# Cross-attention block in fp32 on one core: output projection pair by pair over both tiles, and another order of copies, row sums and one product in the last two attention steps

## The reference, cut to what matters

```python
# x: (2, 2048, 512)  context: (2, 77, 512)  mask: (2, 2048, 77)  H = 16 heads of D = 32
q = layer_norm(x, qn_w, qn_b) @ q_w
k, v = split(layer_norm(context, cn_w, cn_b) @ kv_w)
attn = softmax(where(mask, -FLT_MAX, q . k * D**-0.5))     # per head, 77 keys
x = x + (attn . v) @ proj_w + proj_b
h = gelu(layer_norm(x, n2_w, n2_b) @ fc1_w + fc1_b) @ fc2_w + fc2_b      # 512 -> 2048 -> 512
return x + h
```

## Time and profile before

| | |
|---|---|
| median of three executions | 1068.85 us (1067.42 to 1070.12) |
| the profiled execution, its own time | 1066.18 us |
| its span, first to last instruction | 1064.4 us |
| TensorE busy in the span | 97% |
| VectorE busy | 78% |
| mean granted TensorE clock | 0.995 |

### The profile page before, as it was taken

The page is one execution under the profiler, slowest core; times in us unless marked ns, Lnnn a source line. Parts: engine busy times, 40 slices in busy tenths (PEclk is TensorE's granted clock), DMA queues, the critical chain, the costliest instruction groups (busy, mean ns, idle before and its releaser), DMA issues.

```text
span 1064.4 us, 16336 instructions
## 1 busy us (share of the span) xinstructions
PE 1037.7 (97%) x5857; PEld 856.4 (80%) x5857; DVE 834.3 (78%) x1323; ACT 434.0 (41%) x766; POOL 356.5 (33%) x259
## 2 busy tenths in 40 slices
PE   8999999999999989999999999999999999999998
PEld 6787788888888767887778888887888888888887
DVE  7888989999898789888887666677776677666655
ACT  4343334544434555454453333442433443223221
POOL 2455566665778645232614000302200120400000
PEclk8999999999999999999999999999999999999999
DMA  7012112211210065744477435435635433834312
GB/s 263 9 45 70 50 54 84 86 60 61 80 62 22 21 237 193 262 169 158 180 294 258 184 125 214 157 131 193 261 118 194 161 121 146 316 119 178 113 76 80
DMA packets 52279, 149.19 MB, mean 140 GB/s; under 512 B 10801, under 2 KB 19033, under 8 KB 44019
## 3 DMA queue, kind: packets, MB, share of 16 engines
q1 hardware_dynamic: 51627, 147.25, 38.4%
q10 hardware_dynamic: 584, 1.06, 0.3%
HBM read 108.13 MB, written 39.85 MB: 139 GB/s over the span
## 4 chain that ended last, share of the span: by engine, by line
PE 67%; DVE 18%; DMA 6%; issue 5%; POOL 3%; ACT 1%; DVEq 0%; SPq 0%; POOLq 0%; ACTq 0%
PE bank L1789 28%; PE bank L1759 25%; PE bank L1638 6%; DMA xr<-in_x 3%; DVE xhat L1208 3%; DMA x_scratch<-xr 2%; PE bank L1593 2%; DVE nmax L1160 2%; DVE esum L1185 2%; PE bank L1574 1%; DVE S L1153 1%; DVE aTl L1180 1%; DVE bnst L1196 1%; DVE hring L1374 1%; PE bank L1768 1%
## 5 line engine op out<-in xcount | busy, mean ns | idle before, releaser
L1789 PE MATMUL bank<-w2r,gT 128*128 128x512 f32 x1536 | 360.0, 391 | 2.6 <-DVE acc L1398 2.4
L1789 PEld LDWEIGHTS bank<-w2r,gT 128*128 128x128 f32 x1536 | 286.7, 188 | 64.8 <-DVE acc L1398 6.0
L1759 PE MATMUL bank<-hop,w1r 128*128 128x512 f32 x1344 | 313.5, 392 | 1.3 <-POOL w2r L776 1.3
L1759 PEld LDWEIGHTS bank<-hop,w1r 128*128 128x128 f32 x1344 | 252.5, 189 | 54.5 <-issue 2.1
L1398 DVE TENSOR_TENSOR acc<-bank,acc 128x512 f32<-128x512 f32 x256 | 176.5, 691 | 103.1 <-PE bank L1789 98.3
L1385 DVE TENSOR_TENSOR ybuf<-bank,ybuf 128x512 f32<-128x512 f32 x224 | 148.3, 688 | 71.6 <-PE bank L1759 67.2
L1036 ACT ACTIVATE ybuf<-ybuf,cols 128x512 f32<-128x512 f32 x128 | 91.7, 716 | 162.9 <-DVE ybuf L1385 162.9
L1390 DVE TENSOR_TENSOR gT<-ybuf,gT 128x512 fp32r<-128x512 f32 x128 | 101.7, 816 | 0.0
L676 POOL TENSOR_TENSOR S<-S,rsum 128x1232 f32<-128x1232 f32 x32 | 74.4, 2326 | 63.6 <-DVE rsum L1190 63.6
L641 POOL TENSOR_TENSOR hrs<-hve,mhalf 128x1 f32<-128x1 f32 x32 | 18.0, 562 | 220.1 <-DVE hve L1370 220.1
L669 POOL TENSOR_TENSOR S<-S,nmax 128x1232 f32<-128x1232 f32 x32 | 72.1, 2252 | 35.7 <-DVE nmax L1160 35.4
(11 more groups left out here) (111 smaller groups left out, 1432.0 us busy)
## 6 DMA issues: line engine op xcount, KB each, us to landing
w1r<-w_scratch SPq DMA_DIRECT2D x24, 1792.0 KB, 7.3
w2r<-w_scratch SPq DMA_DIRECT2D x24, 1024.0 KB, 5.2
w_scratch<-w1r SPq DMA_DIRECT2D x8, 1792.0 KB, 6.3
xr<-in_x SPq DMA_DIRECT2D x16, 512.0 KB, 4.1
x_scratch<-xr SPq DMA_DIRECT2D x16, 512.0 KB, 2.8
hring<-x_scratch SPq DMA_DIRECT2D x32, 256.0 KB, 3.0
acc<-x_scratch SPq DMA_DIRECT2D x32, 256.0 KB, 3.8
w_scratch<-w2r SPq DMA_DIRECT2D x8, 1024.0 KB, 9.1
```

The lines of the kernel that those rows point to most:

```text
L1759: mm = pe.matmul(bank_[:, :], w1r[:, w1_slot(s), c, w, kk * P:(kk + 1) * P], hop[i][:, d, kk, :], start=(kk == 0 and n == 0), stop=(kk == ...
L1789: mm = pe.matmul(bY[t % 2][:, :], gT[s % 2][:, j, d, t * P:(t + 1) * P], w2r[:, s % 2, j, w, :], start=(n == 0), stop=(n == 5))
```

## The change

TensorE: `proj` takes the pair as well, and a step runs pair 0 of tile 0, pair 0 of tile 1, pair 1 of tile 0, pair 1 of tile 1 (six matmuls each, in all 24 as before); the banks of both tiles are open at once, and tile 0 is announced as done after the 18th matmul, where it was after the 12th. This holds for all 16 steps. In step 15 the first feed-forward product M1 stands ahead of `prob_T(0)`.

ScalarE, step 14: `prob_out(1)` stands ahead of `exp_all(0)`, where it stood behind it (in step 15 nothing lies between the two places).

VectorE, step 14: `exp_sum(0)` and `recip(0)` ahead of `av_lo(1)`, where they were behind it; `w1_lo(0, 0)` right behind `av_lo(1)`, ahead of `exp_sum(1)`; `hop_lo(0, 1)` ahead of `residual(0)`, where it was between the two residuals.

```diff
@@ ScalarE, step
             if back and (tail == 1 or tail == 2):
                 av_hi(0)
+                prob_out(1)
             if scores:
                 exp_all(0)
             if back and not (tail == 1 or tail == 2):
                 av_hi(0)
-            if back:
                 prob_out(1)
@@ VectorE, step
             if tail == 1:
+                exp_sum(0)
+                recip(0)
                 av_lo(1)
+                w1_lo(0, 0)
...
-            if scores:
+            if scores and tail != 1:
                 exp_sum(0)
                 recip(0)
...
             if tail == 1:
-                w1_lo(0, 0)
+                hop_lo(0, 1)
...
             if back:
                 residual(0)
-            if tail == 1:
-                hop_lo(0, 1)
@@ TensorE, step
-            def proj(t):
+            def proj(pair, t):
                 bank_ = proj_bank(t, scores)
-                if t == 0 and scores:
+                if pair == 0 and t == 0 and scores:
                     v_scores.wait(pe, s, UT * KT - 1)
-                terms = [(c, w, d) for pair in range(PR) for lo in (HI, LO) for c in (2 * pair, 2 * pair + 1)
-                         for w, d in PRODUCTS if d == lo]
+                terms = [(c, w, d) for lo in (HI, LO) for c in (2 * pair, 2 * pair + 1) for w, d in PRODUCTS if d == lo]
                 for n, (c, w, d) in enumerate(terms):
                     if t == 0 and c % 2 == 0 and w == HI:
-                        (a_av, v_av)[d].wait(pe, b, c // 2)
+                        (a_av, v_av)[d].wait(pe, b, pair)
                     mm = pe.matmul(bank_[:, :], aT[d][:, c, t * P:(t + 1) * P], wp[w][:, c, :],
-                                   start=(n == 0), stop=(n == len(terms) - 1))
-                mm.then_inc(t_proj.sem, 1)
+                                   start=(pair == 0 and n == 0), stop=(pair == PR - 1 and n == len(terms) - 1))
+                if pair == PR - 1:
+                    mm.then_inc(t_proj.sem, 1)
...
+            if tail == 2:
+                mul(0, 0, M1, first=True)
             if back:
                 prob_T(0)
             if tail == 2:
-                mul(0, 0, M1, first=True)
                 mul(0, 0, M2, first=True)
...
             if back:
-                proj(0)
-                proj(1)
+                for pair in range(PR):
+                    proj(pair, 0)
+                    proj(pair, 1)
```

## The result

The changed kernel takes 1056.26 us (median of four executions, 1053.02 to 1058.94), where the kernel before took 1068.13 beside it (1065.94 to 1070.12): a ratio of 0.9892, 95% interval 0.9864 to 0.9921, 11.9 us. A second set of six executions gave 1057.22 us and 0.9891 (0.9865 to 0.9917). The profiled execution took 1055.71 us.

What follows compares the result with a forecast made beforehand. It took the attention stage as bound by TensorE with VectorE close behind, and TensorE as 99% busy from 388 us. 7.3 + 4.9 = 12.2 us off the 1068.85 us median gave 1056.7 us, range 1053.5 to 1063.

Steps and rivals of the forecast that it cites:

- Part 1: Projection pair by pair in the attention steps: the wait for aTl goes, 7.3 us gained (bounds nothing and 10 us).
- (a): Limit at score(0, 1), which waits for residual(0) on VectorE: it can come 0.7 us earlier.
- (b): Limit over VectorE from score(0, 1) to the end of residual(0): period not under 21.3 us, from 22.03; again 0.7 us.
- the ring: VectorE's loop from score(0, 1) to the end of residual(0), 21.20 us, of which TensorE shortens nothing.
- 0.65 for each of ten steps: Projection gain per step before step 14: 0.65 us in ten steps, with 0.4 us in two more.
- excess of 1.52 us: Worst-stalling step: projection to next score product took 7.11 us, 1.52 over 5.59; its gain is capped by the residual.
- Part 2: Reordering of steps 14 and 15: M2 ends and av(0) starts earlier, 4.9 us taken (bounds 2.8 and 5.4).
- two orders: Step 14: hop_lo(0, 1) or probs(1) goes first; av(0) of step 15 starts 5.4 or 4.5 us earlier.
- 1.9 us for the copies: Step 14: copies ahead of exp_all(0) shorten the 2.15 us wait of av(1) by 1.9 us (bounds 1.2 and 2.15).
- slow clock: Granted clock of 0.50 at M1 and M2 of step 15: expected not to return; otherwise some 1.7 us lost again.
- What moves with it: Feed-forward from 388 us: every engine keeps its order and TensorE's lead is carried through, cost nothing.
- rival (3): Tail's gain lost to a load or the first feed-forward block: 7.3 us alone, 1061.5 us, chance 0.07.

Runs made afterwards that it cites:

- p1: Kernel before with only the projection pair by pair, order of the last two steps unchanged: 1060.6 us, ratio 0.9932.
- p7: Changed kernel with residual(0) held until the whole projection ends (24th matmul, not 18th): 1064.25 us, ratio 0.9956 against the kernel before.
- p5: Changed kernel with hop_lo(0, 1) of step 14 back between the two residuals: 1055.53 us (single execution).
- p11: Changed kernel with GpSimd's projection bias addition in step 14 moved behind its first subtraction: 1052.85 us (one execution).
- p4: Changed kernel with the copies of pair 1 of step 14 behind the exponential again: 1057.29 us (four executions).
- p3: Changed kernel with M1 of step 15 behind the transposes of pair 0 again: 1059.94 us (median of nine executions).
- p6: Changed kernel with step 14's tile 0 row sums behind av_lo(1) and w1_lo(0, 0) behind both row sums, as before: 1066.5 us (single execution).
- p9: Changed kernel with VectorE's layer norm statistics behind masked(1, 2) and masked(1, 3) ahead of the variance: 1057.24 us, ratio 0.9882 against the kernel before.
- c2: Repeat of the changed kernel with M2 of step 15 also ahead of pair 0's transposes and av_lo(0) earlier on VectorE: 1055.67 us, ratio 0.9891.

## Why the prediction was right, and where it was off

**Part 1, sign and mechanism: right.** I had taken the wait of the 11th matmul away by making it the 17th. In the loop every projection of the changed kernel runs through in 5.56 to 5.60 us, but for one of 5.75, and p1 shows that this alone is worth the 6 us. The period of 21.3 us came as well: six of the thirteen are 21.27 to 21.47 us; five are longer (21.69 to 22.77) and the last two shorter (21.0), as one was before. The prediction had three limits within 0.1 us of each other, TensorE, (a) and (b), and the trace can't rank them in every step. Where TensorE has no idle time its own work is the limit; the ring is seen to bind only where TensorE waits at `score(0, 1)`, in three steps, and p7 doesn't show more.

**Part 1, size: 7.3 predicted, 6.0 in the trace beside it, 6.5 over all traces.** The term that was too large is "0.65 for each of ten steps". In the six ordinary steps that I took for the pattern it is right: 21.97 us on average before (179 to 290 us), 21.34 over the like steps of p5. But the step with an excess of 1.52 us gained nothing beyond its cap (its period, read at the second score product, fell by 0.46 us, from 23.54 to 23.08) and TensorE still waits 1.3 us for `aTl` of pair 0 ahead of `av(1)`, and the step with the first weight sums on GpSimd has 22.62 us before and 22.0 to 23.1 in seven of the ten traces with the new order. In single steps VectorE still waits up to 3.0 us for x: one such wait of 1.71 us at 184 us made a period of 22.77 in the changed kernel. As I read it, its room for them was the wait before `residual(1)`, and that is gone; no run shows this by itself. I had listed the transfer as something that "moves with the step" and forgot that it varies.

**Part 2: 4.9 predicted, 4.35 measured.** Of my two orders the first came: `hop_lo(0, 1)` 1.16 us, `probs` 3.10 us behind it. Against the first score product of step 14, M2 starts after 19.95 us, where that order gave 19.5, and `av(0)` after 21.52, where it gave 20.8. Against the 5.4 us that this order had in the sum, 1.05 are missing. The half microsecond before M2 is the longer `hop_lo(0, 0)`, a lock that I had not looked for since that instruction doesn't move; p11 takes it away. M2 takes 1.57 us where the sum had 1.3, and a further 0.3 us is lost behind `av(0)`, with the wait for `aTl` at 372.92. That 4.9 was near is owed in part to its standing between the two orders. The 1.9 us for the copies measured 1.4 at the end of the stage (p4). The slow clock stayed away, and p3, p5 and p6, where it comes back, show why that was not sure: it hung on M1's place and on VectorE's order as well.

**What moves with it: cost nothing, measured 1.3 us** in feed-forward, in this pair of traces. Not a late load, as in rival (3), but mostly a lock again (below): TensorE has 0.99 us of idle time there that the trace before lacks. There is one trace of the kernel before, and its execution is 2 us under the median, so what the stage costs over many executions is not shown.

The sum of 12.2 us against 11.9 in the medians is thus closer than its terms, and in part by luck: loop and last steps came 1.9 us short in the trace pair, feed-forward took 1.3, and the start gave 1.55 by chance, which makes the 10.6 us of the pair. The 1.3 us by which the medians differ more than the pair lie in executions without a trace.

## What to carry to other kernels

Where two accumulators wait for the same late operand, interleave them: the operand gets the other one's matmuls as cover, and the price is that the first accumulator is done later, so check who reads it. Once a stall is gone, ask what the next limit is before removing another: here TensorE's own work and VectorE's ring both lay at the new period, so holding the residual back cost its whole delay (p7), and p9 only traded one wait for another. When two engines lock each other out, a shift of a few tenths of a microsecond in one stage changes durations in another, so read a gain stage by stage from several traces.

## What the runs showed of the hardware that I had not expected

**The lock decides by hundredths of a microsecond, far from the edit.** The same two instructions in the second weight set of the first block, kernel before:

```profile
435.12 0.68 DVE L1390 TENSOR_TENSOR gT<-ybuf,gT 128x512 fp32r<-128x512 f32 x1
435.14 2.94 POOL L776 TENSOR_TENSOR w2r<-w2raw,w2r 128x1024 fp32r<-128x1024 f32 x1 [7.09 <-ACT w2r L995]
```

and the changed kernel, with TensorE's row behind them:

```profile
423.13 2.40 POOL L776 TENSOR_TENSOR w2r<-w2raw,w2r 128x1024 fp32r<-128x1024 f32 x1 [6.99 <-ACT w2r L995]
423.21 2.87 DVE L1391 TENSOR_TENSOR gT<-ybuf,gT 128x512 fp32r<-128x512 f32 x1
```

```profile
426.74 3.48 PE L1792 MATMUL bank<-w2r,gT 128*128 128x512 f32 x14 [0.99 <-DVE acc L1399]
```

VectorE was first by 0.02 us before, GpSimd by 0.08 us after. The one costs GpSimd 0.5 us that nobody misses, the other holds VectorE for 2.2 us and TensorE for 0.99. The Trainium skill ("SBUF — State Buffer", section "Who interferes with whom") has the rule that the first to start keeps the other out for its whole instruction; the trace agrees.

**Idle time costs the clock in one place and not in the next.** It fell behind 2.15 us in p1 and behind 2.89 us in p3, and behind two shorter idle times close together in p5 (0.71 and 1.12 us) and p6 (0.77 and 1.72 us), but not behind 1.56 us in either trace of the changed kernel, nor behind the 2.13 us of p4, nor behind the 2.15 us ahead of `av(1)` in the kernel before. So the length of one idle time doesn't tell it here. In feed-forward, 42 matmuls behind a wait of 1.32 us took 9.82 us in the changed kernel, and 11.42 us behind a wait of 3.46 us in p6:

```profile
546.30 11.42 PE L1760 MATMUL bank<-hop,w1r 128*128 128x512 f32 x42 [3.46 <-POOL w2r L776]
```

In the second trace of the kernel with M2 ahead (c2), 2.19 us of idle time at 709 us brought no slow clock. Such waits, and the slow clock behind them where it falls, make up the difference between the 671 and the 680 us that this stage takes in the traces though its code never changes: p6 has 5.0 us more idle time there than the kernel before, and about 3.4 us of slow clock (summed over the stretches with a granted clock under 1.00). Whether they also make the spread of some 5 us between executions, and which execution gets them, was not settled.
